# Layer 2's softmax sums by a product with ones held in the array, their reciprocals spread by VectorE's block transposes, in a four-layer graph network on one Trainium2 core

## The reference

```python
def _gat(inp, adj_mask, W, a):
    h = jnp.matmul(inp, W)
    f1 = jnp.matmul(h, a[:F_, 0])
    f2 = jnp.matmul(h, a[F_:, 0])
    e = jax.nn.leaky_relu(f1[:, :, None] + f2[:, None, :], ALPHA)
    if adj_mask is not None:
        e = jnp.where(adj_mask[None, :, :] > 0, e, NEG_INF)
    att = jax.nn.softmax(e, axis=2)
    h_prime = jnp.einsum('bij,bjf->bif', att, h)
    return jax.nn.elu(h_prime)
out = jax.nn.relu(jnp.matmul(x, mlp1_w) + mlp1_b)
residual = out
out = _gat(jax.nn.relu(out), None, W_fc, a_fc)
out = jax.nn.elu(out) + residual
...
```

## Time and profile before

| | before |
|---|---|
| median of 3 runs | 2783.66 us |
| lowest and highest | 2769.3 and 2788.16 us |
| profiled execution, its span | 2787.8 us |
| PE busy, PEld busy | 2604.3 (93%), 2453.2 (88%) |
| DVE busy | 2308.8 us (83%) |
| ACT, POOL busy | 1985.1 (71%), 1959.6 us (70%) |
| DMA | 329.67 MB, mean 118 GB/s |
| chain that ended last | PE 34%, DVE 29%, POOL 13%, issue 10%, ACT 7%, DMA 5% |

### The profile page before, as it was taken

How to read it: one execution, slowest core, us unless ns; L and a number is a source line. 1 busy time by engine, 2 the same in 40 slices (tenths; PEclk the granted TensorE clock), 3 DMA queues, 4 the chain that set the end, 5 groups by cost and what they waited for, 6 DMA issues and landing times.

```text
span 2787.8 us, 64765 instructions
## 1 busy us (share of the span) xinstructions
PE 2604.3 (93%) x21448; PEld 2453.2 (88%) x21448; DVE 2308.8 (83%) x6124; ACT 1985.1 (71%) x4801; POOL 1959.6 (70%) x2439
## 2 busy tenths in 40 slices
PE   4789999999999999999999999999999999999864
...
DVE  2468888888888988888898898888889888888764
...
PEclk7799999999999999999999999999999999999986
...
GB/s 129 49 59 116 136 116 135 116 134 113 126 130 118 133 114 137 112 124 131 123 128 118 131 116 129 123 130 121 118 136 116 127 120 132 120 118 118 95 95 87
DMA packets 317114, 329.67 MB, mean 118 GB/s; under 512 B 35312, under 2 KB 248688, under 8 KB 316784
## 3 DMA queue, kind: packets, MB, share of 16 engines
...
## 4 chain that ended last, share of the span: by engine, by line
PE 34%; DVE 29%; POOL 13%; issue 10%; ACT 7%; DMA 5%; SPq 1%; POOLq 0%; DVEq 0%; ACTq 0%
PE ps L287 22%; POOL xn L1149 6%; DVE att L998 4%; PE ps L526 4%; DMA x0Tp<-in_xT 4%; DVE p L1102 3%; DVE att L993 3%; PE ps L297 3%; DVE p L1087 3%; POOL act L1159 3%; DVE ex L989 2%; DVE act L936 2%; ACT act L605 2%; POOL rstd L1144 2%; PE ps L303 2%
## 5 line engine op out<-in xcount | busy, mean ns | idle before, releaser
L1212 POOL TENSOR_TENSOR p<-p,rd 128x512 f32<-128x512 f32 x256 | 271.8, 1062 | 20.1
L1137 POOL TENSOR_TENSOR x0Tp_lo<-x0Tp,x0Tp_hi 128x512 fp32r<-128x512 f32 x64 | 82.6, 1291 | 288.0 <-ACT x0Tp_hi L542 288.0
L773 ACT ACTIVATE p<-p,nmx 128x256 f32<-128x256 f32 x512 | 256.0, 508 | 12.2 <-DVE nmx L1087 12.2
L1149 POOL TENSOR_SCALAR xn<-act,nmean,rstd 128x256 f32<-128x256 f32 x384 | 237.8, 629 | 23.6 <-POOL rstd L1144 22.5
L287 PE MATMUL ps<-h_lo,proT_hi 128*128 128x256 f32 x512 | 161.0, 314 | 62.9 <-POOL proT_lo L1137 61.9
L1087 DVE CUSTOM_DVE_ANT_0 p<-ps,mask 128x256 f32<-128x256 f32 x512 | 189.3, 417 | 31.2 <-PE ps L500 30.5
L542 ACT ACTIVATE h_hi<-ps 128x512 fp32r<-128x512 f32 x192 | 114.5, 596 | 123.2 <-PE ps L287 123.2
L1137 POOL TENSOR_TENSOR proT_lo<-sco,proT_hi 128x512 fp32r<-128x512 f32 x128 | 166.2, 1299 | 49.4 <-ACT proT_hi L542 49.3
L555 ACT ACTIVATE sco<-sco,nmax 128x256 f32<-128x256 f32 x384 | 190.8, 502 | 7.2 <-DVE nmax L859 6.5
L1159 POOL TENSOR_TENSOR act<-act,x 128x512 f32<-128x512 f32 x64 | 82.9, 1296 | 151.8 <-ACT act L605 151.8
L865 DVE STREAM_TRANSPOSE act<-sco 128x512 f32<-128x512 f32 x192 | 133.2, 694 | 57.2 <-ACT sco L555 56.3
...
## 6 DMA issues: line engine op xcount, KB each, us to landing
scratch<-p SPq DMA_DIRECT2D x128, 512.0 KB, 2.9
p4T<-scratch SPq DMA_DIRECT2D x512, 128.0 KB, 3.4
scratch_pro<-act SPq DMA_DIRECT2D x192, 256.0 KB, 2.4
...
o3r<-scratch_o SPq DMA_DIRECT2D x256, 64.0 KB, 2.1
```

The costliest lines, as they stand in the source:

```text
L773: ins = nc.scalar.activation(rows_, rows_, ACT.Exp, scale=-1.0, bias=nmx4[:, h, m:m + 1], accum_out=den4[:, h, m:m + 1])
L1137: return G.tensor_tensor(lo, whole, hi.bitcast(fp32), ALU.subtract)
L1149: ins = G.tensor_scalar(xn[:, m, :], y[:, m, :], nmean[i][:, m:m + 1], rstd[i][:, m:m + 1], ALU.add, ALU.mult)
L1212: G.tensor_tensor(rows_, rows_, rd4[:, h, :].unsqueeze(2).unsqueeze(3).broadcast_to([P, NT, QUADS, CT * QP]), ALU.mult).then_inc(S["p4n"], 1)
```

## The change

What is computed for the sums is the same, with the operands the other way round. PE's `d2` now holds an array full of ones (128x128) as weights and streams `pfcp`, 256 columns, in 4 matmuls; each partition of the bank then holds the sums for all 256 i. VectorE transposes that row by 32x32 blocks (`dent`, from PSUM), takes the reciprocals of 8 columns of it (`q2`), and spreads them with a second block transpose whose input is a broadcast (`rb2`). PE's and ScalarE's `b2` are gone. `w2` now waits for `dent` to leave bank 5. All five orders are new.

```diff
@@ ORDERS (one line of five)
-    "po": "l0:1 t1:4 t0:2 d40:8 p40:8 m2:5 d41:8 p41:8 d42:8 p42:8 d43:8 p43:8 t3:7 v4:9 y1:4 a0:2 n4:9 v1:4 n1:4 v3:7 n3:7 m3:6 v0:2 k4:7 n0:2 w2:5",
+    "po": "n4:9 m3:6 v0:2 n0:2 k4:7 w2:5 l0:0 t1:3 m2:4 d40:7 p40:7 d41:7 p41:7 d42:7 p42:7 d43:7 t0:1 t3:6 p43:7 y1:3 a0:1 v1:3 n1:3 v3:6 n3:6 v4:8",
...
-        ones2 = sb("ones2", [P, 2], f32r)
+        ones2 = sb("ones2", [P, P], f32r)
...
-        rdc = sb("rdc", [P, NT])
+        dent = sb("dent", [P, N // QP, QP])
+        rdc = sb("rdc", [P, N // QP])
...
 PE
             def d2(t):
 
                 pe.wait_ge(S["pfcl"], t + 1)
-                enter(5, "rdc", t + 1)
-                for m in range(NT):
-                    for k in range(NT):
-                        for i in (1, 0):
-                            ins = nc.tensor.matmul(ps[:, 5, 2 * m:2 * m + 2], pfcp[i][:, k, m * P:(m + 1) * P], ones2[:, :],
-                                                   start=(k == 0 and i == 1), stop=(k == NT - 1 and i == 0))
+                enter(5, "dent", t + 1)
+                for k in range(NT):
+                    for i in (1, 0):
+                        ins = nc.tensor.matmul(ps[:, 5, 0:N], ones2[:, :], pfcp[i][:, k, :], start=(k == 0 and i == 1), stop=(k == NT - 1 and i == 0))
                 ins.then_inc(S["d2_mm"], 1)
-
-            def b2(t):
-                pe.wait_ge(S["rdc"], t + 1)
-                enter(5, "rdb", t + 1)
-                spread(ps[:, 5, N:2 * N], lambda m: rdc[:, m:m + 1]).then_inc(S["b2_mm"], 1)
...
 ACT
-            def b2(t):
-                ac.wait_ge(S["b2_mm"], t + 1)
-                wait(ac, S["att"], t)
-                copy(rdb[:, :], ps[:, 5, N:2 * N]).then_inc(S["rdb"], 1)
...
 DVE
-                V.tensor_copy(ones2[:, :], ones[:, :])
+                V.tensor_copy(ones2[:, :], ones[:, 0:1].broadcast_to([P, P]))
...
             def d2(t):
                 dv.wait_ge(S["d2_mm"], t + 1)
-                wait(dv, S["b2_mm"], t)
-                V.reciprocal(rdc[:, :], ps[:, 5, 0:4:2]).then_inc(S["rdc"], 1)
+                wait(dv, S["rdb"], t)
+                V.transpose(dent[:, :, :].rearrange("p c j -> p (c j)"), ps[:, 5, 0:N]).then_inc(S["dent"], 1)
+
+            def q2(t):
+                dv.wait_ge(S["dent"], t + 1)
+                V.reciprocal(rdc[:, :], dent[:, :, 0]).then_inc(S["rdc"], 1)
+
+            def b2_(t):
+                dv.wait_ge(S["rdc"], t + 1)
+                wait(dv, S["att"], t)
+                V.transpose(rdb[:, :], rdc[:, :].unsqueeze(2).broadcast_to([P, N // QP, QP])).then_inc(S["rdb"], 1)
```

More of the change, by code:

```diff
@@ L161, in graph_stack @@
  xn0 xnT0_mm xnT0h xnT0 h1_mm h1h h1 f1_mm raw1 nmax1 pro1 rden1 pro1_x pro1_dma proT1h proT1 av1_mm act1 cl1 q1 y1 mv1 rstd1
- xn1 xnT1_mm xnT1h xnT1 o1_mm o1T o1Th o1Tl hfc_mm hfch hfc f2_mm fmax lrow ef u pfc pfch pfcl d2_mm rdc b2_mm rdb v2_mm w2_mm att ex1 cut2 ex2 res o2 o2Th o2T
+ xn1 xnT1_mm xnT1h xnT1 o1_mm o1T o1Th o1Tl hfc_mm hfch hfc f2_mm fmax lrow ef u pfc pfch pfcl d2_mm dent rdc rdb v2_mm w2_mm att ex1 cut2 ex2 res o2 o2Th o2T
  o3_mm o3T o3Th o3Tl o3_x o3_dma h3_mm h3h h3 f3_mm raw2 nmax2 pro2 rden2 pro2_x pro2_dma proT2h proT2 av3_mm act2 cut3 ex3 cl3 q3 r3 y2 mv2 rstd2
```

6 lines of the change are left out of this document (3 added, 3 removed), and 8 rows, old and new, of the table ORDERS.

## The result

| | changed kernel | before |
|---|---|---|
| median | 2633.97 us (4 runs) | 2784.64 us (4 runs) |
| lowest and highest | 2628.76 and 2636.18 us | 2769.3 and 2788.16 us |
| ratio, 95% interval | 0.9473 [0.9444, 0.9502] | |

The change makes the kernel 5.3% faster.

The account below looks back on a forecast made before the run. The prediction took PE to bound the round. Savings of 0.61 (PE's own work), 0.22 (`xn`) and 0.25 (`proT_lo`) sum to 1.08 us a round, times 64 is 69 us: 2787.8 - 69 = 2718.7 us, range 2685 to 2768.

Parts of the forecast that it names:

- The direct saving on PE: PE's stretch from the first sums matmul to the scores: 4.56 us falls to 3.95, saving 0.61 us a round (0.5 to 0.7).
- The waits: PE's waits for `proT_lo` (0.50 us a round) and `xn` (0.22): 0.25 of the first and all of the second saved.
- half of the wait for `proT_lo`: PE's wait ahead of `a3`: half of its 0.50 us a round taken as recovered, 0.25 us.
- The order that it set out for GpSimd: GpSimd after the fourth reciprocal: a 128x2 product (0.20 us), `t0` (1.3), then `t3` (1.3), ending at about 1451.6.
- `xn`: PE's wait for the normalized `xn`, 0.22 us a round, goes with 1.4 us to spare, as `n4` leaves GpSimd's chain.
- the straight line: VectorE's transpose time scaled from 512 and 1024 elements: 0.44 us for 256 elements (bounds 0.35 and 0.70).
- The cover: VectorE's added 0.8 us a round is hidden by PE's own work; without that it costs the whole 0.8 us.
- The wait for the DMA of `x0Tp`: ScalarE's 1.55 us wait for x transposed goes, since that DMA is issued without waiting for VectorE's transposes.
- The filling: Start of the kernel: shorter through the earlier DMA; the prediction is wrong if it changes by more than 15 us.
- B: Rival: only PE's own work is saved and the waits stay, 39 us less, 2749 us; chance 0.27.
- C: Rival: no gain, VectorE's path to `att` becomes the bound, `att` 0.6 us late, 2788 us; chance 0.16.
- D: Rival: slower, `t0` and `t3` queue behind `d43` on GpSimd, `a3` 1.6 us later, 2852 us; chance 0.07.

Follow-up runs that it names:

- the old addresses: The changed kernel with all tiles that both kernels have at their SBUF addresses of before: 2643.58 us, ratio 0.9508 to the kernel before.
- Experiments 11: The changed kernel with `t3` put back behind `p43` on GpSimd: 2725.72 us, ratio 0.9819 to the kernel before.
- 12: The kernel of experiment 3 with `t3` moved ahead of `p43` on GpSimd and ahead of `k2` on ScalarE: 2743.2 us, ratio 0.9874 to the kernel before.
- experiment 10: The changed kernel with the last layer's `v4` and `n4` back at their old places on GpSimd, and VectorE's `ag4` too: 2662.24 us, 0.9589 of before.
- experiment 3: The kernel before with the new sums and new addresses, in the old orders without `b2`: 2758.81 us, ratio 0.9921 to the kernel before.
- experiment 4: The changed kernel with the old sums in the new orders, at the new addresses, PE's `b2` behind `v4`: 2739.48 us, 0.9857 of the kernel before.

## Why the prediction was right or wrong, point by point

**The direct saving on PE**, 0.61 us (0.5 to 0.7): with the old addresses 0.71 in a typical round and 0.60 in the mean, with the new ones 0.82 and 0.69. The kind was right to the instruction: four rows 0.12 us apart, 0.20 behind the transpose, 0.55 in all (0.56 said). With the old addresses `v4` took 1.43 (1.44 said), `n2` 1.52 (1.54 said) and the transposes of `x0` 0.36 (0.41 said). `v4` and `n2` gained another 0.12 from the addresses, which were not thought of. Two terms were left out: 0.08 that comes back at `f3`, since the stretch was counted from its first row and not from `f3`, and about 0.1 for the rounds with a wait for `nmax`. Two-column matmuls at the price of a whole load each were right.

**The waits: the step that failed.** The prediction sized them by the idle time in the PE rows, 0.50 and 0.22, called the load rows (1.14 together) an upper bound, and then took half of the first. They cost 1.02 from start to start, and all of it went. Of the 1.13 us a round by which the sum of 1.08 fell short of 2.21, this term is 0.55 (1.02 against 0.47). The other steps, for which the sum had nothing, are 0.38, and the addresses, which it did not have either, 0.21; the direct saving, by its mean, is 0.01 the other way. In microseconds: 139 + 17 measured against 69 predicted.

**Why half of the wait for `proT_lo`.** The prediction set the end of `t3` against the fourth reciprocal and found it no earlier. Its rows came from the graph around 1450 us, where `a0` took 1450.23 to 1451.87 = 1.64 us; in the five others between 1400 and 1620 us it took 1.64, 2.24, 2.25, 2.34 and 2.46. The row stood for the mildest case. The order that it set out for GpSimd was what happened (GpSimd, then PE, of the changed kernel):

```profile
1517.10 0.20 POOL L1203 TENSOR_TENSOR rd<-some,den 128x2 f32<-128x2 f32 x1
1517.25 1.30 POOL L1135 TENSOR_TENSOR gT_lo<-sco,gT_hi 128x512 fp32r<-128x512 f32 x1
1518.51 1.31 POOL L1135 TENSOR_TENSOR proT_lo<-sco,proT_hi 128x512 fp32r<-128x512 f32 x1
...
1518.85 0.28 PE L288 MATMUL ps<-h_lo,gT_hi 128*128 128x256 f32 x1
...
1520.29 0.28 PE L288 MATMUL ps<-h_lo,proT_hi 128*128 128x256 f32 x1
```

`gT_lo` ends 0.30 us before `a0` starts and `proT_lo` 0.47 before `a3`. What came earlier is VectorE's fourth reciprocal. From the start of the multiplication into `att` to its end it was 7.17 us before and 5.93 in the change (medians between 400 and 2400 us), 1.24 less. By their means `i2` is 0.49 us shorter, as said (0.5), but `n2` is 0.72 shorter too, which the prediction did not count; of the other steps between two left and two came, which about cancels. The row of `n2` before, to be held against that of L987:

```profile
L989 DVE TENSOR_SCALAR ex<-ex x64: 667/1452/1456, 153.1 to 2695.5; 128x1024 f32<-128x1024 f32 x64
```

So the reciprocal comes earlier by about the 1.3 us that `t0` costs in its new place ahead of `t3`, and what `t3` gained by going ahead of `p43` is left whole. Experiments 11 and 12 bear this out from either side: with the reciprocal at 5.93 and `t3` behind `p43` the wait is back, and with the reciprocal as late as before (7.22) but `t0` not ahead of `t3`, it is nearly gone. Why `n2` and `i2` became shorter no experiment took apart.

**`xn`.** The wait went, as said, but with 0.73 us to spare and not 1.4, and not for the reason given alone: 0.43 of it is `f2`, which now stands ahead of `x1`. Putting `n4` back did not bring the wait back; what it cost, 0.45 us a round, fell elsewhere (experiment 10).

**VectorE.** The transposes took 0.44 us each, as the straight line said; PE did not wait for `dent` to leave the bank, and VectorE waited for the sums in one round of 64. The cover that the prediction asked for held.

**ScalarE.** The wait for the DMA of `x0Tp` is gone, as said.

**The filling.** The sign was right. Filling and draining together came to 17 us, over the 15 that were named as the point where the prediction would be wrong; the filling alone, up to the first reciprocal, was 12 us.

**The rivals.** B in its pure form is experiment 3, but worse than priced: with the old orders over half of PE's saving came back as a wait and 11 us were left, not 39. C did not happen: `att` starts at 1549.10 behind scores that started at 1548.73, 0.37 us (before 1482.50 - 1482.06 = 0.44). D did not happen, as the margins of 0.30 and 0.47 us show. `gT_lo` held PE up three times in 52 rounds, by 1.8 us at most.

**What stays open.** Which moves besides `t3` and `n4` matter: each line put back, and each move carried into the old table, gave a new wait. It is shown that the gain belongs to sums and table together (11 and 31 us apart, 136 together), and that 26 of the 94 us between are experiment 4's badly placed `b2`; how the rest divides is not. And what shortens `f1`, `a3`, `m3` and the other small steps is open.
